# Row maxima of an attention written into the bf16 operand by GpSimd in place of small transfers

## The chip, the cores and the metric

The program runs on one core of one Trainium2 chip, and nothing runs beside it. The metric is the device time of the core in microseconds (us). Before the change the median of three runs is 3215.1 us (3196.7 to 3217.6).

## What is computed

Three layers over x of 2048 positions and 128 channels: a recurrent mixing layer with a mixture-of-experts block behind it, a latent attention, and the same block again. Both blocks (called F and H in the trace) hold a full attention with 16 heads of 8 channels; the latent attention (L) is causal and is brought to the same form. The mixing layer's names begin with R, the experts' with FE and HE. Cut to what matters here:

```python
# F and H: full, once for each of the two blocks
scores = jnp.einsum('bqhd,bkhd->bhqk', q, k) / jnp.sqrt(jnp.float32(Dh))
attn = jax.nn.softmax(scores, axis=-1)
ctx = jnp.einsum('bhqk,bkhd->bqhd', attn, v).reshape(Bb, Ss, Dd)

# L: causal
attn = jnp.einsum('bhql,bkl->bhqk', q_lat, c_kv) / sqrt(hs)
attn = jnp.where(causal[None, None], attn, -jnp.inf)
attn = jax.nn.softmax(attn, axis=-1)
```

The softmax needs the maximum over all keys of each query before the exponential. The kernel computes each score twice: once with the queries on the partitions, to take the maxima, and once with the keys on the partitions, to take the exponential and weigh the values.

## The kernel before

`attention` (lines 89 to 576) is built three times, as F, L and H. Each build has two blocks.

**The first block** (lines 146 to 230) projects queries and keys and splits each float32 into three bf16 parts. The parts go through DRAM (`qscr`, `kscr`) into the operands `qa` and `ka`, 128 partitions by three slots (one for a head) by 2048 columns. A head fills 48 rows (six products of parts by 8 channels), once from partition 0 and once from partition 64, so that two row groups can be multiplied from different rows of the array. GpSimd fills the whole of `ka` with -1 (line 191) and then `vstack` with 1 (line 192); SyncE stores the parts, and issues `load_q` for head 0 once the query parts are stored.

**The second block** (from line 310) runs the heads. A head has 64 max items in F and H (40 in L): TensorE multiplies 128 queries by up to 512 keys into one of three PSUM buffers (line 440), and VectorE reduces it (line 536). It has two halves `a` of 1024 queries. When all maxima of a half are there, VectorE makes `top`, GpSimd splits it into three bf16 parts `topp` (lines 511 to 521, four small operations), TensorE turns `topp` (the "turn" item, line 431), VectorE copies it into `toprow` (line 533), and SyncE writes it with six DMAs (`tops`, lines 316 to 324) into rows 48 to 50 and 112 to 114 of `qa`. `ka` holds -1 there, so that the score matmul over 51 rows (line 401) yields score minus maximum. The first score of each half waits for those DMAs (`top_in`, line 393). ScalarE takes the exponential of 1024 columns (line 497), and TensorE weighs the values (line 419), eight instructions a key tile.

**The order.** Every engine runs its list in order. The max items of the next head are spread between the scores of the current one: `LEAD` (lines 258 to 261) is the number of max items that stand ahead of a head's first score, chosen as the smallest for which each turn lies `MARGIN` cost units ahead of the score that needs it. With 3600, `LEAD` is 44 in F and H, and 42 in L. In L the turn of half 1 of a head and the turn of half 0 of the next head stand 13 items apart; in F and H, 33. TensorE's list loops four times over three heads (line 470), with the first three heads and the last outside the loop. SyncE's list for a head in F and H is: loads of q, k and v two heads on, `spread` (five DMAs for the outputs of the head before), `tops` of half 1, `keep`, `tops` of half 0 of the next head. In the middle of a head VectorE also divides the outputs of the head before (`divide`, lines 547 to 552).

Of the kernel before, what the change touches and what calls it, by code (L numbers as in the profile page):

```python
# [12 lines left out]
P = 128  # L13
# [41 lines left out]
SROWS = MAIN + PARTS  # L55
# [33 lines left out]
def attention(nc, name, xT, wq, wk, wv, consts, out_yT, causal):  # L89
# [3 lines left out]
    zero_rows = consts["zero_rows"]  # L93
    qscr = nc.dram_tensor(name + "_qparts", (PARTS, P + DH, T), BF16, kind="Internal").ap()
# [8 lines left out]
    topp = heads.enter_context(nc.sbuf_tensor(name + "topp", [P, P // 8, 8], BF16))  # L103
# [8 lines left out]
    kept = semaphore(nc, heads, name + "kept")  # L112

    loaded = [semaphore(nc, heads, f"{name}loaded{s}") for s in range(SLOTS)]
    LOADS = 16 * (2 * GROUPS * PARTS + 1)
    FIRST_ROW = [sum(PARTS - b for b in range(a)) * DH for a in range(PARTS)]
# [19 lines left out]
    with ExitStack() as ctx:  # L136
# [17 lines left out]
        with nc.Block() as block:  # L154
# [33 lines left out]
            @block.gpsimd  # L188
            def _(pool):

                nc.gpsimd.memset(ka[:, :, :], -1.0).then_inc(filled, 1)
                nc.gpsimd.memset(vstack[:, :, :, :], 1.0).then_inc(ones, 1)
                nc.gpsimd.memset(topp[:, :, :], 0.0).then_inc(filled, 1)
                nc.gpsimd.memset(nothing[:, :], 0.0).then_inc(filled, 1)
                pool.wait_ge(filled, 3)
# [13 lines left out]
            def _(sp):  # L209
# [8 lines left out]
                sp.sem_inc(kept, 16)  # L218
                for scr in (qscr, kscr):
# [5 lines left out]
                sp.wait_ge(q_stored, 32)  # L225
                load_q(sp, 0, 0)
# [31 lines left out]
    MARGIN = 3600  # L258
# [30 lines left out]
    with heads as ctx:  # L289
# [21 lines left out]
        TOPS = 16 * PARTS * GROUPS  # L311

        with nc.Block() as block:
            @block.sync
            def _(sp):
                def tops(h, a, s, c):

                    sp.wait_ge(max_free, c)
                    for r in range(GROUPS):
                        cols = slice(a * HALF + r * BANK, a * HALF + (r + 1) * BANK)  # L320
                        for part in range(PARTS):
                            row = 64 * r + MAIN + part
                            sp.dma_start(qa[row:row + 1, s, cols].rearrange("o (t q) -> o t q", t=4),
                                         toprow[part * 8 + 4 * r:part * 8 + 4 * r + 4, :]).then_inc(top_in, 16)

# [18 lines left out]
                tops(0, 0, 0, count(0, 0, "turn"))  # L344

                def head(h, u, first=False, last=False):
                    if causal:
                        tops(h, 1, u % SLOTS, count(h, 1, "turn"))
                        if not first:
                            spread(h - 1)  # L350
# [8 lines left out]
                    if not causal:  # L359
                        tops(h, 1, u % SLOTS, count(h, 1, "turn"))  # L360
                    if not first:
                        keep(h - 1)
                    if not last:
                        tops(h + 1, 0, (u + 1) % SLOTS, count(h + 1, 0, "turn"))
# [17 lines left out]
            def _(pe):  # L382
# [7 lines left out]
                def score(h, s, a, n):  # L390

                    if n == 0:
                        pe.wait_ge(top_in, (2 * h + a + 1) * TOPS)
                    done = h * NS + a * NSCORE[0] + n
                    pe.wait_ge(expd, done + 1)
                    for i, (kt, q0, q1) in enumerate(SCORES[a][n]):
                        r = q0 // BANK
                        rows = slice(64 * r, 64 * r + SROWS)
# [25 lines left out]
                def item(h, s, a, j, out, c):  # L424
# [4 lines left out]
                    if j == "turn":  # L429
                        pe.wait_ge(top_split, 2 * h + a + 1)  # L430
                        nc.tensor.transpose(out[:, 0:P // 2].bitcast(BF16), topp[:, :, :].rearrange("p a t -> p (a t)"),
# [5 lines left out]
                    rows = slice(64 * r, 64 * r + MAIN)  # L437
# [72 lines left out]
            def _(pool):  # L510
                def split_maxima(h, a):
                    u = 2 * h + a
                    pool.wait_ge(topped, u + 1)
                    nc.gpsimd.tensor_tensor(topp[:, 0, :], top[:, 0, :], nothing[:, :], ALU.add).then_inc(chain, 1)
# [1155 lines left out]
```

## Time and profile before

| what | us |
|---|---|
| median of three runs | 3215.1 |
| the profiled execution | 3210.3 |
| its span, from first to last instruction | 3208.5 |
| TensorE busy in the span | 2795.7 (87%) |
| VectorE busy | 2123.1 (66%) |
| ScalarE busy | 1714.2 (53%) |
| GpSimd busy | 214.6 (7%) |
| second block of F | 503 to 1262 |
| second block of L | 1585 to 2092 |
| second block of H | 2178 to 2935 |

The three attentions take about 2020 us of the 3208. Busy time of TensorE is modelled and its matmuls overlap. The granted clock is the share of TensorE's full 2.4 GHz; 0.50 is its lower level, 1.2 GHz.

### The profile page before, as it was taken

What the parts mean: (1) busy time and instruction counts of PE and PEld (TensorE: products, weight loads), DVE (VectorE), ACT (ScalarE), POOL (GpSimd) and SP (SyncE); (2) the same over time, 40 slices, a digit from 0 to 9 for tenths busy, and PEclk for the clock granted to TensorE, in tenths of its full rate; (3) what the DMA queues carried; (4) which work ended last, traced back from release to release, by engine and by line L of the source; (5) the groups of instructions that cost most, each with busy time, mean ns of one, the idle gap of its engine ahead of it and who ended that gap; (6) DMA issues with size and microseconds to landing.
All of it is one profiled execution on the core that took longest, in us unless ns stands there. A gap on an engine that the chain in (4) does not pass through costs nothing. (4 is left out here: it accounts for less than half of the span.)

```text
span 3208.5 us, 62945 instructions
## 1 busy us (share of the span) xinstructions
PE 2795.7 (87%) x20985; PEld 1217.1 (38%) x20985; DVE 2123.1 (66%) x4016; ACT 1714.2 (53%) x2055; POOL 214.6 (7%) x469
## 2 busy tenths in 40 slices
PE   6788857999999997999599999939998989896998
PEld 2688842222222232444244444422222223222443
DVE  5544467988888894322578777648988979784222
ACT  4222223776677676433166656624776767675343
POOL 1222210000000000000100000010000000000000
PEclk8888856998898898899699999967989989888999
DMA  1000001110110110211111111110111011010211
GB/s 43 1 0 0 0 17 65 36 33 22 36 35 23 34 36 22 78 41 39 69 40 47 53 38 53 48 65 30 32 36 33 24 35 35 20 36 22 79 59 33
DMA packets 89023, 115.82 MB, mean 36 GB/s; under 512 B 19645, under 2 KB 62615, under 8 KB 86383
## 3 DMA queue, kind: packets, MB, share of 16 engines
q1 hardware_dynamic: 85561, 110.38, 11.2%
q8 instruction: 181, 2.97, 0.4%
q10 hardware_dynamic: 3248, 2.21, 0.3%
q14 instruction: 33, 0.27, 0.0%
HBM read 78.39 MB, written 20.55 MB: 31 GB/s over the span
## 5 line engine op out<-in xcount | busy, mean ns | idle before, releaser
L536 DVE TENSOR_REDUCE Hmaxes<-Hm 128x1 f32<-128x512 f32 x1024 | 626.8, 682 | 108.5 <-PE Hm L440 108.4
L536 DVE TENSOR_REDUCE Fmaxes<-Fm 128x1 f32<-128x512 f32 x1024 | 626.5, 682 | 99.3 <-PE Fm L440 99.3
L497 ACT ACTIVATE Hprob<-Hs 128x1024 f32<-128x1024 f32 x512 | 522.4, 1025 | 208.2 <-PE Hs L401 165.2
L497 ACT ACTIVATE Fprob<-Fs 128x1024 f32<-128x1024 f32 x512 | 522.4, 1025 | 200.7 <-PE Fs L401 158.4
L536 DVE TENSOR_REDUCE Lmaxes<-Lm 128x1 f32<-128x512 f32 (+3 forms) x640 | 354.2, 605 | 111.9 <-PE Lm L440 54.5
L497 ACT ACTIVATE Lprob<-Ls 128x1024 f32<-128x1024 f32 (+7 forms) x384 | 294.1, 777 | 182.3 <-PE Ls L401 99.0
L419 PE MATMUL Fo<-Fprob,Fvh 128*32 128x256 f32 x4096 | 339.9, 419 | 0.3 <-ACT Fprob L497 0.3
L419 PE MATMUL Ho<-Hprob,Hvh 128*32 128x256 f32 x4096 | 337.8, 416 | 0.3 <-ACT Hprob L497 0.3
L440 PE MATMUL Hm<-Hka,Hqa 48*128 48x512 bf16 x1024 | 291.7, 419 | 42.7 <-DVE Hmaxes L536 16.5
L440 PE MATMUL Fm<-Fka,Fqa 48*128 48x512 bf16 x1024 | 294.1, 422 | 38.3 <-DVE Fmaxes L536 15.4
L401 PE MATMUL Hs<-Hqa,Hka 51*128 51x512 bf16 x1024 | 246.6, 407 | 34.6 <-DMA Hqa<-Htoprow 27.6
L401 PE MATMUL Fs<-Fqa,Fka 51*128 51x512 bf16 x1024 | 247.3, 410 | 26.7 <-DMA Fqa<-Ftoprow 25.1
L440 PE MATMUL Lm<-Lka,Lqa 48*128 48x512 bf16 (+3 forms) x640 | 201.9, 377 | 31.6 <-DMA Lvh<-Lvstack 14.2
L419 PE MATMUL Lo<-Lprob,Lvh 128*32 128x256 f32 (+1 forms) x2688 | 211.4, 360 | 0.0
L440 PEld LDWEIGHTS Hm<-Hka,Hqa 48*128 48x128 bf16 x1024 | 83.7, 94 | 312.5 <-DVE Hmaxes L536 152.8
L440 PEld LDWEIGHTS Fm<-Fka,Fqa 48*128 48x128 bf16 x1024 | 84.1, 95 | 310.5 <-DVE Fmaxes L536 157.3
L401 PE MATMUL Ls<-Lqa,Lka 51*128 51x512 bf16 (+3 forms) x640 | 166.0, 362 | 3.4 <-ACT Lprob L497 3.3
L419 PEld LDWEIGHTS Ho<-Hprob,Hvh 128*32 128x32 f32 x4096 | 91.6, 113 | 196.4 <-ACT Hprob L497 106.3
L419 PEld LDWEIGHTS Fo<-Fprob,Fvh 128*32 128x32 f32 x4096 | 92.0, 113 | 190.8 <-ACT Fprob L497 108.2
L794 ACT ACTIVATE FEhid<-FEh,FEb1p 128x512 f32<-128x512 f32 x128 | 87.8, 687 | 124.4 <-PE FEh L749 123.7
L794 ACT ACTIVATE HEhid<-HEh,HEb1p 128x512 f32<-128x512 f32 x128 | 87.6, 687 | 124.3 <-PE HEh L749 123.5
L858 DVE SCALAR_TENSOR_TENSOR HEpart<-HEy,cols,HEwb 128x512 f32<-128x512 f32 x32 | 24.0, 751 | 160.0 <-PE HEy L760 153.2
(426 smaller groups left out, 3072.2 us busy)
## 6 DMA issues: line engine op xcount, KB each, us to landing
FEwb<-FE_weights SPq DMA_DIRECT2D x8, 1024.0 KB, 5.5
HEwb<-HE_weights SPq DMA_DIRECT2D x8, 1024.0 KB, 5.5
Fvh<-Fvstack SPq DMA_DIRECT2D x17, 256.0 KB
Lvh<-Lvstack SPq DMA_DIRECT2D x17, 256.0 KB
Hvh<-Hvstack SPq DMA_DIRECT2D x17, 256.0 KB
FEw<-in_L_ffn_W SPq DMA_DIRECT2D x16, 256.0 KB, 2.9
HEw<-in_L_ffn_W SPq DMA_DIRECT2D x16, 256.0 KB, 2.9
Fqa<-F_qparts SPq DMA_DIRECT2D x34, 96.0 KB
```

What stands on the lines that cost most here:

```text
L401: last = nc.tensor.matmul(sps[n % 2][:, o:o + q1 - q0], ka[rows, s, kt * P:(kt + 1) * P], qa[rows, s, a * HALF + q0:a * HALF + q1], start= ...
L419: last = nc.tensor.matmul(ops[VW * g:VW * (g + 1), j * P:2 * P], vh[:, s, kt * VW:(kt + 1) * VW], p[:, j:2, g * P:(g + 1) * P], start=(kt ...
L440: m = nc.tensor.matmul(out[:, 0:n], qa[rows, s, qt * P:(qt + 1) * P], ka[rows, s, lo:lo + n], start=True, stop=not diag)
L497: nc.scalar.activation(prob[:, :, :].rearrange("p k q -> p (k q)")[:, lo:hi], sps[n % 2][:, o:o + hi - lo], ACT.Exp, scale=SCALE).then_inc ...
L536: nc.vector.reduce_max(maxes[:, a, t, half:half + 1], src[:, 0:w], AX.X).then_inc(max_free, 1)
L794: nc.scalar.activation(hid[:, k % 2, f, :], hps[f][:, :], ACT.Gelu_apprx_tanh, bias=b1p[:, (k // NB) * FC + f:(k // NB) * FC + f + 1])\
L858: nc.vector.scalar_tensor_tensor(out=part[:, k % 2, :], in0=yps[k % YSLOTS][:, :], scalar=b2T[:, bass.ds(i * 2 + u, 1)], in1=wb[:, u, cols ...
```

## The change

Rows. A row group of `qa` and `ka` now begins with twelve rows for the maxima (`TROWS`), four for each part, and the 48 rows of the head follow from row 12. Row 4·part+t holds the maxima in the 128 columns of query tile t of its 512 columns, and zero in the others. Both matmuls run over 60 rows.

Writing. Instead of six DMAs GpSimd multiplies `toprow` (twelve rows, broadcast four times) by `pick` (0 or 1) into 12 rows by 512 columns, twice for each half, once in each row group. The second does not wait for the first.

Clearing. The max matmuls read the maxima's rows too, so those have to be zero before a head's max items. GpSimd clears them for the head two on, with `ka` minus `ka` into 12 rows by 2048 columns, twice for each head (14 heads), in its list between the maxima of half 1 and those of half 0 of the next head. TensorE waits for it (`cleared`) before a head's first max item.

Filling. In the first block GpSimd fills 32 partitions by 6144 columns four times (`ka` and `qa`, each row group) where it filled 128 partitions once, and waits for all four before `vstack`; SyncE waits for them before `load_q` of head 0.

Lead. `MARGIN` becomes 4100 in L, where `LEAD` stays 42 and the order stays, and 5200 in F and H, where `LEAD` becomes 47. SyncE's list loses `tops`.

```diff
-SROWS = MAIN + PARTS
+TROWS = 4 * PARTS
+ROWS = TROWS + MAIN
...
-                nc.gpsimd.memset(ka[:, :, :], -1.0).then_inc(filled, 1)
+                for r in range(GROUPS):
+                    nc.gpsimd.memset(ka[64 * r:64 * r + 32, :, :], -1.0).then_inc(filled, 1)
+                    nc.gpsimd.memset(qa[64 * r:64 * r + 32, :, :], 0.0).then_inc(filled, 1)
+                pool.wait_ge(filled, 4)
                 nc.gpsimd.memset(vstack[:, :, :, :], 1.0).then_inc(ones, 1)
...
                 sp.wait_ge(q_stored, 32)
+                sp.wait_ge(filled, 4)
                 load_q(sp, 0, 0)
...
-    MARGIN = 3600
+    MARGIN = 4100 if causal else 5200
...
-                def tops(h, a, s, c):
-                    sp.wait_ge(max_free, c)
-                    for r in range(GROUPS):
-                        cols = slice(a * HALF + r * BANK, a * HALF + (r + 1) * BANK)
-                        for part in range(PARTS):
-                            row = 64 * r + MAIN + part
-                            sp.dma_start(qa[row:row + 1, s, cols].rearrange("o (t q) -> o t q", t=4),
...
-                        pe.wait_ge(top_in, (2 * h + a + 1) * TOPS)
+                        pe.wait_ge(top_in, (2 * h + a + 1) * GROUPS)
...
-                    rows = slice(64 * r, 64 * r + MAIN)
+                    rows = slice(64 * r, 64 * r + ROWS)
...
+                                pe.wait_ge(cleared, 2 * (h + 1))
...
+                def maxima(h, a, s, c):
...
+                    pool.wait_ge(max_free, c)
+                    for r in range(GROUPS):
+                        rows = slice(64 * r, 64 * r + TROWS)
+                        cols = slice(a * HALF + r * BANK, a * HALF + (r + 1) * BANK)
+                        nc.gpsimd.tensor_tensor(qa[rows, s, cols].rearrange("k (t q) -> k t q", t=4),
+                                                toprow[rows, :].unsqueeze(1).broadcast_to([TROWS, 4, P]),
+                                                pick4(r), ALU.mult).then_inc(top_in, 1)
+                    pool.wait_ge(top_in, GROUPS * (u + 1))
+
+                def clear(h, s):
+
+                    pool.wait_ge(weighed, RING + NK * h)
+                    for r in range(GROUPS):
+                        rows = slice(64 * r, 64 * r + TROWS)
+                        nc.gpsimd.tensor_tensor(qa[rows, s, :], ka[rows, s, :], ka[rows, s, :], ALU.subtract)\
+                            .then_inc(cleared, 1)
+                    pool.wait_ge(cleared, 4 + GROUPS * h)
+
+                def head(h, u, first=False, last=False):
+                    maxima(h, 1, u % SLOTS, count(h, 1, "turn"))
+                    if not first and not last:
+                        clear(h, (u + 2) % SLOTS)
+                    if not last:
+                        maxima(h + 1, 0, (u + 1) % SLOTS, count(h + 1, 0, "turn"))
```

A table `pick` of four columns is loaded with the other constants and copied to bf16 once.

## Rows read from the trace of the kernel before

**Rows 1.** The page's costliest groups: the score matmuls of H; idle before, releaser.

```profile
L401 PE MATMUL Hs<-Hqa,Hka 51*128 51x512 bf16 x1024 | 246.6, 407 | 34.6 <-DMA Hqa<-Htoprow 27.6
```

**Rows 2.** Busy time in stretches: two heads of F, two of L; clock behind POOL.

```profile
631.10:674.10 43.00, 40.49 (x391) 12.36 (x387) 40.63 (x70) 33.16 (x35) 1.61 (x8) 1.00 0.10 31
910.80:959.50 48.70, 43.63 (x387) 13.74 (x386) 40.77 (x70) 33.20 (x35) 1.60 (x8) 0.89 0.11 32
1735.20:1764.20 29.00, 28.14 (x316) 12.88 (x314) 23.89 (x49) 18.73 (x26) 1.61 (x8) 1.00 0.18 50
1764.20:1800.30 36.10, 32.22 (x316) 14.62 (x314) 24.10 (x48) 18.89 (x26) 1.60 (x8) 0.86 0.15 42
```

**Rows 3.** Timeline (start, length, instruction) of VectorE: half 0's maxima, heads 1 and 16.

```profile
546.06 0.18 DVE L544 TENSOR_REDUCE Ftop<-Fmaxes 128x8 f32<-128x32 f32 x1
...
1238.68 0.19 DVE L544 TENSOR_REDUCE Ftop<-Fmaxes 128x8 f32<-128x32 f32 x1
...
2211.20 0.19 DVE L544 TENSOR_REDUCE Htop<-Hmaxes 128x8 f32<-128x32 f32 x1
...
2912.24 0.19 DVE L544 TENSOR_REDUCE Htop<-Hmaxes 128x8 f32<-128x32 f32 x1
```

**Rows 4.** Timeline of TensorE: first scores of half 1 in two heads of F.

```profile
638.74 0.39 PE L401 MATMUL Fs<-Fqa,Fka 51*128 51x512 bf16 x2 [0.53 <-DMA Fqa<-Ftoprow]
...
729.29 0.39 PE L401 MATMUL Fs<-Fqa,Fka 51*128 51x512 bf16 x2 [1.00 <-DMA Fqa<-Ftoprow]
```

**Rows 5.** Timeline ahead of the second of them: the copy, and SyncE's six DMAs.

```profile
723.68 0.22 DVE L533 COPY Ftoprow<-Fm 128x128 bf16<-128x128 bf16 x1
...
724.29 3.86 SPq L323 DMA_DIRECT2D Fqa<-Ftoprow  x6
```

**Rows 6.** Timeline of VectorE: the division in a head's middle, the reduction behind it.

```profile
637.68 0.94 DVE L549 RECIPROCAL Fsums<-Fsums 128x128 f32<-128x128 f32 x1
...
638.98 1.28 DVE L536 TENSOR_REDUCE Fmaxes<-Fm 128x1 f32<-128x512 f32 x2
```

**Rows 7.** Timeline of VectorE: a max item behind the first score of half 0.

```profile
618.86 1.29 DVE L536 TENSOR_REDUCE Fmaxes<-Fm 128x1 f32<-128x512 f32 x2 [0.36 <-PE Fm L440]
```

**Rows 8.** Timeline of the first block of F: GpSimd's fill, SyncE's first loads.

```profile
469.54 5.22 POOL L191 MEMSET Fka<- 128x6144 bf16 x1 [55.28 <-POOLq L592]
...
482.92 3.95 SPq L124 DMA_DIRECT2D Fqa<-F_qparts  x6
...
496.42 3.89 SPq L132 DMA_DIRECT2D Fka<-F_kparts  x6
```

**Rows 9.** Groups by form: elementwise work on GpSimd, and on VectorE with 64 partitions and 128.

```profile
L1000 POOL TENSOR_TENSOR RvT<-RvT,Rmix_k 128x2048 f32<-128x2048 f32 x1 | 4.5, 4519 | 0.1
L1110 POOL TENSOR_TENSOR RXT<-RMB,tab 128x512 f32<-128x512 f32 x8 | 10.2, 1270 | 191.6 <-DVE RMB L1188 191.6
L1169 DVE SCALAR_TENSOR_TENSOR RAR<-Rkk,RT 64x512 f32<-64x512 f32 x8 | 5.5, 686 | 0.2
L1206 DVE TENSOR_TENSOR RX<-Rq,RX 128x512 f32<-128x512 f32 x32 | 22.1, 692 | 67.9 <-PE Rq L1241 67.9
```

**Rows 10.** Timeline of GpSimd: two fills with no wait between them.

```profile
0.28 0.10 POOL L1658 MEMSET const-float32-1.0<- 128x1 f32 x1
0.32 0.10 POOL L1658 MEMSET const-bfloat16-1.0<- 128x1 bf16 x1
```

**Rows 11.** Timeline of L: from the turn of half 1 to the next head's turn.

```profile
1699.45 0.23 DVE L533 COPY Ltoprow<-Lm 128x128 bf16<-128x128 bf16 x1
...
1706.45 0.20 POOL L514 TENSOR_TENSOR Ltopp<-Ltop,Lnothing 128x8 bf16<-128x8 f32 x1 [8.12 <-DVE Ltop L542]
...
1707.29 0.20 POOL L520 TENSOR_TENSOR Ltopp<-Ltop,Ltopp 128x8 bf16<-128x8 f32 x1
...
1708.36 0.23 PE L431 MATMUL Lm<-ident_bf,Ltopp 128*128 128x128 bf16 x1 [0.29 <-DVE Lmaxes L536]
```

**Rows 12.** Timeline of TensorE: its loop's second pass in L begins.

```profile
1787.62 0.22 PE L440 MATMUL Lm<-Lka,Lqa 48*128 48x128 bf16 x1 [3.09 <-issue]
```

More of the change, by code:

```diff
@@ L93, in attention @@
     zero_rows = consts["zero_rows"]
+    pick = consts["pick_bf"]
     qscr = nc.dram_tensor(name + "_qparts", (PARTS, P + DH, T), BF16, kind="Internal").ap()
@@ L102, in attention @@
     ka = heads.enter_context(nc.sbuf_tensor(name + "ka", [P, SLOTS, T], BF16))
-    topp = heads.enter_context(nc.sbuf_tensor(name + "topp", [P, P // 8, 8], BF16))
+    topp = heads.enter_context(nc.sbuf_tensor(name + "topp", [P, GROUPS, P // 8, 4], BF16))
     nothing = heads.enter_context(nc.sbuf_tensor(name + "nothing", [P, 8], F32))
@@ L112, in attention @@
     kept = semaphore(nc, heads, name + "kept")
+    cleared = semaphore(nc, heads, name + "cleared")
     loaded = [semaphore(nc, heads, f"{name}loaded{s}") for s in range(SLOTS)]
     LOADS = 16 * (2 * GROUPS * PARTS + 1)
-    FIRST_ROW = [sum(PARTS - b for b in range(a)) * DH for a in range(PARTS)]
+    FIRST_ROW = [TROWS + sum(PARTS - b for b in range(a)) * DH for a in range(PARTS)]
     def load_q(sp, h, s):
@@ L218, in _ @@
                 sp.sem_inc(kept, 16)
+                sp.sem_inc(cleared, 4)
                 for scr in (qscr, kscr):
@@ L343, in _ @@
                     load_kv(sp, h, h)
-                tops(0, 0, 0, count(0, 0, "turn"))
                 def head(h, u, first=False, last=False):
[L347 to L350, printed above, removed]
+                    if causal and not first:
+                        spread(h - 1)
                     if not last:
@@ L436, in item @@
                     r = kb % GROUPS
-                    rows = slice(64 * r, 64 * r + MAIN)
+                    rows = slice(64 * r, 64 * r + ROWS)
                     lo = kb * BANK
@@ L510, in _ @@
             def _(pool):
-                def split_maxima(h, a):
+                pick4 = lambda r: pick[64 * r:64 * r + TROWS, :].unsqueeze(2).broadcast_to([TROWS, 4, P])
+                def maxima(h, a, s, c):
                     u = 2 * h + a
+                    halves = lambda x: x.rearrange("p (r t) -> p r t", r=GROUPS)
+                    high, middle, low = (topp[:, :, part, :] for part in range(PARTS))
                     pool.wait_ge(topped, u + 1)
-                    nc.gpsimd.tensor_tensor(topp[:, 0, :], top[:, 0, :], nothing[:, :], ALU.add).then_inc(chain, 1)
+                    nc.gpsimd.tensor_tensor(high, halves(top[:, 0, :]), halves(nothing[:, :]), ALU.add).then_inc(chain, 1)
@@ L515, in split_maxima @@
                     pool.wait_ge(chain, u * 3 + 1)
-                    nc.gpsimd.tensor_tensor(top[:, 1, :], top[:, 0, :], topp[:, 0, :], ALU.subtract).then_inc(chain, 1)
+                    nc.gpsimd.tensor_tensor(halves(top[:, 1, :]), halves(top[:, 0, :]), high, ALU.subtract)\
+                        .then_inc(chain, 1)
                     pool.wait_ge(chain, u * 3 + 2)
-                    nc.gpsimd.tensor_tensor(topp[:, 1, :], top[:, 1, :], nothing[:, :], ALU.add).then_inc(chain, 1)
+                    nc.gpsimd.tensor_tensor(middle, halves(top[:, 1, :]), halves(nothing[:, :]), ALU.add).then_inc(chain, 1)
@@ L519, in split_maxima @@
                     pool.wait_ge(chain, u * 3 + 3)
-                    nc.gpsimd.tensor_tensor(topp[:, 2, :], top[:, 1, :], topp[:, 1, :], ALU.subtract)\
-                        .then_inc(top_split, 1)
-                with pool.Fori(0, NH) as h:
-                    for a in range(2):
-                        split_maxima(h, a)
+                    nc.gpsimd.tensor_tensor(low, halves(top[:, 1, :]), middle, ALU.subtract).then_inc(top_split, 1)
+                    pool.wait_ge(max_free, c)
[5 more added lines that the diff above has]
+                                                pick4(r), ALU.mult).then_inc(top_in, 1)
@@ L527, in _ @@
+                maxima(0, 0, 0, count(0, 0, "turn"))
+                for u in range(SLOTS):
+                    head(u, u, first=(u == 0))
+                with pool.Fori(1, (NH - 1) // SLOTS) as i:
+                    for u in range(SLOTS):
+                        head(i * SLOTS + u, u)
+                head(NH - 1, 0, last=True)
             @block.vector
@@ L1432 @@
 CONSTS = [("ident", P), ("eye2", HS), ("mpair", 2 * P), ("levels", LEVELS * P), ("level0t", P), ("blockones", P),
-          ("iota", E_N)]
+          ("iota", E_N), ("pick", 4)]
 MASKS = [("ident2", 2 * P), ("mask2_kq", 2 * P), ("mask2_qk", 2 * P)]
@@ L1457, in constant_table @@
         "mask2_qk": folded(np.where(r > c, BIG, 0.0)),
+        "pick": np.where(r % 64 < TROWS, r % 4 == np.arange(4)[None, :], 0.0),
         "iota": np.broadcast_to(np.arange(E_N)[None, :], (P, E_N)),
@@ L1532, in build @@
         consts["ident_bf"] = sb("ident_bf", [P, P], BF16)
+        consts["pick_bf"] = sb("pick_bf", [P, 4], BF16)
         for n in ("ident2_bf", "mask2_kq_bf", "mask2_qk_bf"):
```

18 lines of the change are left out of this document (6 added, 12 removed).

## The prediction

> **What bounds the kernel now.** I read the costliest groups first, to see what TensorE waits for. In H its score matmuls sit idle for 27.6 us behind the DMAs that bring the maxima [rows 1]; F shows 25.1 us, L nothing. That is under 1 us a half, and by itself small. So I looked next at single heads, in the stretches. A head of F at full clock takes 43.0 us, with VectorE busy for 40.6 of it: VectorE, with its 64 reductions, sets the pace, and TensorE at 40.5 us is just behind it [rows 2]. But most heads are not like this one. From head 1's maxima to head 16's, fifteen heads take 692.6 us in F and 701.0 us in H [rows 3], where fifteen of 43.0 would take 645. The reader is to ask where those 48 and 56 us are.
>
> Part is the clock. At the lower level TensorE can't keep VectorE fed. The timeline of TensorE shows when the level falls: the score that opens half 1 waited 0.53 us in an early head, which stayed at full clock, and 1.00 us in a later one [rows 4], and the 9.5 us behind that were granted 0.50. I listed these waits in F as far as the timeline prints them: nine were of 1.00 to 2.21 us, and eight of the nine were followed by a stretch at 0.50 (six of 9 to 10 us, two shorter); three of 0.53 to 0.61 us were followed by none. The wait is long because SyncE is late: the copy into `toprow` ended at 723.90, and the six DMAs began at 724.29 and took 3.86 us to issue [rows 5], behind the loads and `spread`.
>
> The other part is TensorE's loop. Three times in each attention, as its list jumps back, TensorE pauses for some 3.1 us with nothing to wait for [rows 12] and the clock falls behind it. Such a head costs 48.7 us in F (its half 1 kept the full clock), against 43.0, so 5.7 more; in L 36.1 against 29.0, so 7.1 more [rows 2].
>
> **The change part by part, in F and H.** It removes the DMAs and their wait. What stands in their place: GpSimd's two multiplications of 12 by 512. No row shows twelve partitions or bf16 there; the nearest is 1.27 us for 128 by 512 f32 [rows 9]. From the copy's end that makes 0.1 + 2.5 us if one runs behind the other, against 5.4 us from 723.90 to 729.29 [rows 4, 5], and the longer lead gives three max items more, about 1.9 us by 0.64 us an item (1.28 us for two, [rows 6]). So the maxima are there some 4.5 us earlier than now, against waits of at most 2.2 us. The wait is gone. What is late next is the division: VectorE leaves its reductions at 637.68 and comes back at 638.98 [rows 6], and TensorE, three buffers ahead at most, stands still for part of that. It did so in the early head with its wait of 0.53 us, and that head kept its clock [rows 2, 4]. So I take the clock to stay up in half 1 as well. In half 0 a gap of 0.36 us on VectorE goes [rows 7].
>
> A head then takes 43.0 - 0.36 = 42.6 us. Fifteen make 639.0, less 1.0 because the first of them has no division, plus three loop pauses at 5.7 = 17.1: 655.1 us. Against 692.6 and 701.0 [rows 3] that saves 37.5 us in F and 45.9 in H, 83.4 together. The lead costs at the end: the scores trail the last maximum by three items more, 1.9 us each in F and H, 3.8 together. Net 79.6, say 80 us. The bounds: if the wait goes and the lower clock stays, about 30 us (see the rivals); if the loop pauses too lost their low stretch, 5.7 would become 3.1 and six of them give 16 us more.
>
> The clearing, 12 by 2048, is by the nearest row 4.5 us [rows 9], twice. In F and H the next turn's maxima come 28 max items after the copy, over 17 us, and 2.5 + 9.0 us fit in front. Its wait for `weighed` is over by then, and TensorE's wait for `cleared` comes almost a head later. Nothing is queued on GpSimd that anyone needs sooner. 60 rows in place of 48 and 51 stream the same number of columns: nothing. SyncE loses 576 DMA issues in all; it isn't what ends the steady heads once `top_in` doesn't hang on it, and its loads, two heads ahead, come no later: nothing. `pick` costs one small copy at the start: nothing.
>
> **In L** no wait for the maxima exists to be removed and the order stays, so there is only something to lose. Here the clearing sits in a narrow place. The copy of half 1 ended at 1699.68; GpSimd's split for the next head ran from 1706.45 to 1707.49, and TensorE took the turn at 1708.36 [rows 11], 8.7 us behind the copy. Between them GpSimd now has two multiplications, two clearings and the split (1.0 us). If operations on different partitions run one behind the other: 0.1 + 2.5 + 0.1 + 9.0 + 1.1 = 12.8 us, 4.1 us late, and TensorE, in order, stands at the turn with every score, weighing and max item behind it. If the two of a pair overlap: 0.1 + 1.3 + 0.1 + 4.5 + 1.1 = 7.1 us, 1.6 us early, and nothing is lost. So the whole question is whether they overlap. What the trace shows: a fill at 0.28 of 0.10 us, and the next one starting at 0.32 [rows 10], so GpSimd's sequencer doesn't wait for one to end before it starts the next; and these have no semaphore between them, as the new pairs have none. It doesn't show a pair on different partitions. I take the overlap, as the nearer to this row, and keep the other end as a rival.
>
> The Trainium skill's GPSIMD Engine Reference, section 2.1 (Instruction dispatch), says why it could: each of the engine's eight cores serves its own 16 partitions and starts the next instruction once its own share is done, without waiting for the others. Rows 0 to 11 and 64 to 75 belong to different cores, so by that rule the pair costs 4.5 us and L loses nothing, and by a strict order it costs 9.0 us; no row of this trace shows partial partitions on GpSimd, so it stays a rule until one does. The same rule lets no part of a single instruction go faster with twelve partitions than with sixteen.
>
> **The first block.** One fill of 6144 columns takes 5.22 us [rows 8]. Four of 32 partitions: 20.9 us if they run in order with the cost of the whole, 10.4 us if the row groups overlap, 5.2 us or less if the cost goes by partitions (on VectorE 64 partitions cost 686 ns and 128 692 ns [rows 9], so I don't take that for GpSimd either). SyncE would issue `load_q` at 482.92, 13.4 us behind the start of the fill [rows 8]. With 10.4 us it isn't delayed; with 20.9 us it is by 7.5 us, and all that follows up to 496.42 is issued by SyncE one behind the other, so the second block begins 7.5 us later, three times: 22.5 us. `vstack` follows, later than now, but ends before SyncE does in both cases. I take 0, by the same answer as in L.
>
> **The sum.** 3208.5 - 80 = 3128.5 us of span. The profiled execution took 3210.3 us and the median of the runs is 3215.1; 80 off the median is 3135 us, 2.5% less.
>
> **The rivals.** *In order.* GpSimd runs the pairs one behind the other. L: in eleven of the fourteen heads with a clearing TensorE stands for 4.1 us, and the pause of 3.09 us, which cost 7.1 us [rows 2, 12], shows that it doesn't end there: the clock falls and 4.0 us more go. 8.1 × 11 = 89 us; at the three loop pauses the gap is wider already, some 1 us each; together 92. With the 22.5 of the first blocks that is 115 against 80 saved: 3250 us, slower. For it speaks that no row shows an overlap of different partitions; against it the two fills [rows 10]. It decides from where the clearings take more than some 6 us together (8.7 less 0.1, 1.3, 0.1 and 1.1): below that L is untouched.
>
> *The clock stays low.* The wait goes, but the division and the three idle pieces around it still bring the lower level, as one shorter mechanism in half 1. Then only the waits are saved: 0.36 us in half 0 and about 0.9 us in half 1, in some 27 heads, 34, less 3.8: 30 us, 3185. Against it stands the early head, which had the division and stayed up; for it, that the later heads differ in the loads beside them.
>
> *No change at all*, the maxima as late as now because a broadcast, masked write on GpSimd costs several times its nearest row: from 1.27 us each it would have to be 3.5 us in order. Then 3215.
>
> **How the numbers follow.** The forecast (overlap, clock kept) 0.50, its own range 3108 to 3170; the clock stays low 0.22; in order 0.20; no change or a mixture 0.08. A difference under 1%, 32 us, is about what a measurement of this kernel can't tell from none. Faster by over 1%: 0.50, half of the second case and 0.01 of the last, 0.62. Within 1%: the other half and most of the last, 0.17. Slower: 0.21. The range goes from 3108 (forecast with 16 us for the loops and some 10 for the other terms) to 3235, which leaves out most of the in-order case.
>
> **What would show it.** Right: no wait of a score on the maxima; heads of F near 42.6 us at clock 1.00 but for three with a pause; in GpSimd's timeline the second of a pair starting while the first runs; in L 29.0 us a head as before; `load_q` of head 0 no later behind the fill than 13.4 us. Wrong: the turn in L idle behind the split with GpSimd's clearings ahead of it, or fills at a distance of 5.2 us; or stretches of 0.50 in the middle of the heads of F with no wait for maxima ahead of them.

## The result, and the profile after

The change makes the kernel slower: 3329.0 us (median of four runs, 3319.2 to 3335.2) against 3213.0 us (four runs of the kernel before, 3196.7 to 3217.6), a ratio of 1.037, with a 95% interval of 1.032 to 1.041. The forecast was 3135 us, and its range ended at 3235. The profiled execution took 3329.6 us with a span of 3327.9, and its mean granted clock is 0.867 against 0.883 before.

To see where the 119.4 us of span come from, I cut both spans at the first and the last max matmul of each attention. One row a matmul group gives both (shortest, median and longest duration, then first and last start). First the kernel before, then after:

```profile
L440 PE MATMUL Fm<-Fka,Fqa x1024: 372/387/632, 502.8 to 1237.4; 48*128 48x512 bf16 x171
...
L440 PE MATMUL Hm<-Hka,Hqa x1024: 372/387/632, 2167.6 to 2911.0; 48*128 48x512 bf16 x171
...
L440 PE MATMUL Lm<-Lka,Lqa x640: 224/386/631, 1584.4 to 2065.7; 48*128 48x512 bf16 x127, 48*128 48x128 bf16 x16, 48*128 48x384 bf16 x16, 48*128 48x256 bf16 x1
```

```profile
L428 PE MATMUL Fm<-Fka,Fqa x1024: 383/387/631, 507.9 to 1276.9; 60*128 60x512 bf16 x171
...
L428 PE MATMUL Hm<-Hka,Hqa x1024: 376/387/631, 2262.0 to 3031.1; 60*128 60x512 bf16 x171
...
L428 PE MATMUL Lm<-Lka,Lqa x640: 223/386/631, 1629.7 to 2154.2; 60*128 60x512 bf16 x127, 60*128 60x128 bf16 x16, 60*128 60x384 bf16 x16, 60*128 60x256 bf16 x1
```

F grew from 734.6 to 769.0 us, L from 481.3 to 524.5, H from 743.4 to 769.1, and all that lies outside them from 1249.2 to 1265.3: +34.4, +43.2, +25.7 and +16.1, together 119.4. So it isn't one place.

What the change was made for did happen. In the page's costliest groups the score matmuls of H were idle for 34.6 us before [rows 1]; after, no DMA stands among the releasers. A new wait stands in another group, the max matmuls of F, which wait for VectorE's reductions:

```profile
L428 PE MATMUL Fm<-Fka,Fqa 60*128 60x512 bf16 x1024 | 317.1, 431 | 89.4 <-DVE Fmaxes L558 59.9
...
L389 PE MATMUL Hs<-Hqa,Hka 60*128 60x512 bf16 x1024 | 262.2, 409 | 1.7 <-ACT Hprob L486 1.7
```

The list of TensorE's waits in F counts them (waiter, releaser: us, times, longest): 59.9 us, with one as long as 3.4 us.

```profile
PE Fm L428 <- DVE Fmaxes L558: 59.9, 71, 3.4
```

The timeline of the middle of a head of F shows what VectorE does there (start, length, instruction, idle time before it):

```profile
693.20 7.26 POOL L530 TENSOR_TENSOR Fqa<-Fka 12x2048 bf16<-12x2048 bf16 x2 [0.17 <-POOL Fqa L520]
...
696.53 0.95 DVE L571 RECIPROCAL Fsums<-Fsums 128x128 f32<-128x128 f32 x1
...
697.62 2.98 DVE L574 TENSOR_TENSOR Fquot<-Fsums 128x128 f32<-128x128 f32 x1
700.52 3.07 DVE L558 TENSOR_REDUCE Fmaxes<-Fm 128x1 f32<-128x512 f32 x5
701.26 1.20 PE L428 MATMUL Fm<-Fka,Fqa 60*128 60x512 bf16 x2 [3.42 <-DVE Fmaxes L558]
```

GpSimd's two clearings run from 693.20 to 700.46. The quotient, a multiplication of 128 by 128 with both operands in SBUF, starts inside them and is over only at 700.60, right behind their end: 2.98 us. Before, it took 0.29 us. The reciprocal (one operand) keeps its 0.95 us inside the same clearings, and the reductions, whose operand is in PSUM, keep their 0.6 us each. It is so in most heads: the median of 16 is 2980 ns. The quotient's line in before, in F after, and in L after (where it doesn't meet the clearings):

```profile
L552 DVE TENSOR_TENSOR Fquot<-Fsums x16: 291/292/293, 595.8 to 1271.1; 128x128 f32<-128x128 f32 x16
```

```profile
L574 DVE TENSOR_TENSOR Fquot<-Fsums x16: 291/2980/2985, 601.6 to 1309.3; 128x128 f32<-128x128 f32 x16
...
L574 DVE TENSOR_TENSOR Lquot<-Lsums x16: 291/291/295, 1703.0 to 2188.5; 128x128 f32<-128x128 f32 x16
```

TensorE, in order, stands still for 3.42 us, and the clock falls behind it. The first stretch is a whole head of F, the second the 9.8 us in which the wait ends (the clock is the third figure from the end); the third is a head of L. They answer to the heads of 43.0 us at 1.00 and 29.0 us at 1.00 before [rows 2].

```profile
667.40:715.40 48.00, 43.73 (x391) 13.58 (x394) 43.25 (x71) 33.26 (x34) 12.91 (x14) 0.89 0.10 30
700.00:709.80 9.80, 8.54 (x48) 2.24 (x48) 7.27 (x12) 4.43 (x5) 0.45 (x1) 0.50 0.03 8
...
1716.65:1749.94 33.29, 30.61 (x316) 13.07 (x314) 24.39 (x48) 18.86 (x26) 12.91 (x14) 0.90 0.14 43
```

In L it is the other case, the rival called "in order". GpSimd's timeline, and the turn behind it:

```profile
1719.43 2.14 POOL L520 TENSOR_TENSOR Lqa<-Ltoprow,pick_bf 12x512 bf16<-12x512 bf16 x2 [1.35 <-DVE Ltoprow L555]
1721.64 7.26 POOL L530 TENSOR_TENSOR Lqa<-Lka 12x2048 bf16<-12x2048 bf16 x2
1728.98 0.20 POOL L507 TENSOR_TENSOR Ltopp<-Ltop,Lnothing 128x8 bf16<-128x8 f32 x1
...
1729.81 0.20 POOL L514 TENSOR_TENSOR Ltopp<-Ltop,Ltopp 128x8 bf16<-128x8 f32 x1
1730.16 0.22 PE L419 MATMUL Lm<-ident_bf,Ltopp 128*128 128x128 bf16 x1 [2.41 <-POOL Ltopp L514]
```

The groups give the mean of one as 1031 and 3591 ns, so two take 2.14 and 7.26 us: one behind the other, with no overlap to be seen. The turn is 2.41 us late, and a head of L takes 33.3 us.

The first block of F shows the same pattern:

```profile
466.85 5.21 POOL L195 MEMSET Fka<- 32x6144 bf16 x1 [55.04 <-POOLq L614]
472.01 5.21 POOL L196 MEMSET Fqa<- 32x6144 bf16 x1
477.27 5.21 POOL L195 MEMSET Fka<- 32x6144 bf16 x1
482.44 5.21 POOL L196 MEMSET Fqa<- 32x6144 bf16 x1
...
487.74 3.98 SPq L127 DMA_DIRECT2D Fqa<-F_qparts  x6
```

The fills start every 5.2 us, and `load_q` is issued 20.9 us behind the first of them, against 13.4 us before [rows 8].

### The profile page after: what moved, and what is told of

It reads as the page before. It is cut to its first block and busy times, and to the rows that moved or that the text cites. A ratio compares the mean times of both kernels' runs of the same rounds, so it can differ in the third digit from the quotient of the medians.

```text
span 3327.9 us, 62702 instructions
## 1 busy us (share of the span) xinstructions
PE 2834.5 (85%) x20985; PEld 1218.5 (37%) x20985; DVE 2200.0 (66%) x4017; ACT 1714.6 (52%) x2055; POOL 760.6 (23%) x754
## 3 DMA queue, kind: packets, MB, share of 16 engines
q8 instruction: 182, 2.98, 0.4%
## 5 line engine op out<-in xcount | busy, mean ns | idle before, releaser
L428 PE MATMUL Hm<-Hka,Hqa 60*128 60x512 bf16 x1024 | 312.7, 427 | 101.6 <-DVE Hmaxes L558 62.0
L428 PE MATMUL Fm<-Fka,Fqa 60*128 60x512 bf16 x1024 | 317.1, 431 | 89.4 <-DVE Fmaxes L558 59.9
L389 PE MATMUL Fs<-Fqa,Fka 60*128 60x512 bf16 x1024 | 266.5, 414 | 1.7 <-ACT Fprob L486 1.7
L389 PE MATMUL Hs<-Hqa,Hka 60*128 60x512 bf16 x1024 | 262.2, 409 | 1.7 <-ACT Hprob L486 1.7
L428 PE MATMUL Lm<-Lka,Lqa 60*128 60x512 bf16 (+3 forms) x640 | 208.2, 399 | 35.8 <-DMA Lvh<-Lvstack 21.6
L428 PEld LDWEIGHTS Hm<-Hka,Hqa 60*128 60x128 bf16 x1024 | 87.2, 95 | 375.8 <-DVE Hmaxes L558 188.9
L428 PEld LDWEIGHTS Fm<-Fka,Fqa 60*128 60x128 bf16 x1024 | 87.4, 95 | 369.0 <-DVE Fmaxes L558 188.2
L407 PE MATMUL Lo<-Lprob,Lvh 128*32 128x256 f32 (+1 forms) x2688 | 219.4, 373 | 0.0
L389 PE MATMUL Ls<-Lqa,Lka 60*128 60x512 bf16 (+3 forms) x640 | 183.1, 391 | 3.4 <-ACT Lprob L486 3.2
```

What stands on the lines that cost most here:

```text
L389: last = nc.tensor.matmul(sps[n % 2][:, o:o + q1 - q0], ka[rows, s, kt * P:(kt + 1) * P], qa[rows, s, a * HALF + q0:a * HALF + q1], start= ...
L407: last = nc.tensor.matmul(ops[VW * g:VW * (g + 1), j * P:2 * P], vh[:, s, kt * VW:(kt + 1) * VW], p[:, j:2, g * P:(g + 1) * P], start=(kt ...
L428: m = nc.tensor.matmul(out[:, 0:n], qa[rows, s, qt * P:(qt + 1) * P], ka[rows, s, lo:lo + n], start=True, stop=not diag)
```

## The experiments

Theory A: two mechanisms together make the loss, and each can be taken away alone. In F and H the clearing holds VectorE's quotient, and the clock falls behind it; in L, and in the first blocks, GpSimd runs its pairs in order. The rivals are that the loss of F and H comes from something else that the change brought (60 rows instead of 51, the order of SyncE's list, the longer lead), or that the half clock would come anyway. Two of the kernels, before + clearings and before + fills, add work on a tile that nobody reads.

The clearing moved behind the next head's first maxima, 13 items later in L and 33 in F and H (against the changed kernel, as are the next three):

```diff
                     maxima(h, 1, u % SLOTS, count(h, 1, "turn"))
-                    if not first and not last:
-                        clear(h, (u + 2) % SLOTS)
                     if not last:
                         maxima(h + 1, 0, (u + 1) % SLOTS, count(h + 1, 0, "turn"))
+                    if not first and not last:
+                        clear(h, (u + 2) % SLOTS)
```

> The changed kernel with one thing moved: in GpSimd's list the clearing stands behind the maxima of half 0 of the next head, not ahead of them. Theory A (the clearing does the harm by its place: in L it delays the split that the turn waits for; in F and H it lies across VectorE's quotient, a tensor_tensor with two SBUF inputs, which then takes 2.98 us for 0.29 and leaves TensorE standing for 3.4 us): the quotient is back at 0.29 us in F and H, TensorE's wait of 3.42 us is gone, L's heads go from 33.6 back to 29.0 us, and the whole takes some 3225 us. Theory B (the clearing loads SBUF or the power budget wherever it stands, or 60 rows and the longer lead are what costs): L gains its 40 us, F and H nothing, 3285 us.

Measured: 3181.0 us, 0.989 [0.987, 0.991] of before. F is 692.1 us and H 703.5, which is 42.5 and 39.9 less than before and 77 and 66 less than with the change. The quotient is back at 292 ns there. The expectation had some 3225 us, 44 more than came, and L's heads back at 29.0 us, which didn't come: the moved clearings now meet L's quotient, and it takes 2.35 us there.

```profile
1717.85 7.26 POOL L530 TENSOR_TENSOR Lqa<-Lka 12x2048 bf16<-12x2048 bf16 x2 [0.17 <-POOL Lqa L520]
...
1719.22 2.37 DVE L574 TENSOR_TENSOR Lquot<-Lsums 128x128 f32<-128x128 f32 x1
```

In this place the quotient is let go 3.7 us into the 7.26 (1721.59 against 1717.85), at the end of the first of the two clearings (half of 7.26 is 3.63). So it waits for the one instruction that runs when it comes, not for the pair. L is 512.0 us, still 30.7 more than before.

The other side moved, the division six scores later in F and H, with the clearing where the change put it:

```diff
-                        if k == NS // 2 and not first:
+                        if k == NS // 2 + (0 if causal else 6) and not first:
```

> The changed kernel with VectorE's division six score items later in the heads of F and H (at item 22 of 32, not 16), so that it stands some 8 us behind its old place and outside the clearing; GpSimd's list, L and the first blocks are those of the changed kernel. Theory A: the quotient takes 0.29 us, F and H lose 25 to 30 us each against the changed kernel, L stays at 524 us: 3265 to 3280 us. Theory B (contention wherever, rows, lead): 3329 us, with the quotient short but the heads of F still near 48 us.

Measured: 3187.5 us, 0.991 [0.989, 0.993]. F 694.0, H 700.1, and L at 524.3, as slow as with the change. The work is the same, and so are the rows, SyncE's list, the lead and the number of clearings; only where the division stands differs. It brings back 144 us in F and H together (75.0 and 69.0). The median fell by 141 us, more than twice the 49 to 64 that I expected. The 25 to 30 us that I expected for each attention are about 2 us for each of its 14 heads with a clearing, and some 5 us a head came back: the clock's part was missing, and the mean clock of the whole went from 0.867 to 0.900, above the 0.883 of before. The rivals for F and H are out.

The clearing given to SyncE, as two DMAs of zeros for each head:

```diff
+        for r in range(GROUPS):
+            sp.dma_start(qa[64 * r:64 * r + TROWS, s, :], zero_rows[0:TROWS, :]).then_inc(loaded[s], 16)
...
-                    if not first and not last:
-                        clear(h, (u + 2) % SLOTS)
```

> The changed kernel without GpSimd's clearing: the twelve rows of each group are zeroed by two DMAs from a DRAM tensor of zeros, ahead of the loads of q. Theory A: as with the clearing moved, some 3225 us; the two should agree within 10 us, since the clearing behind the next head's maxima touches nothing that waits. Theory B (the clearing costs wherever it stands): clearly faster than with the clearing moved, 3200 us or less.

Measured: 3159.4 us, 0.982 [0.979, 0.985]. F 694.5, L 478.6, H 708.2: both mechanisms gone with the clearings. The expectation was missed: this kernel was to lie within 10 us of the one with the clearing moved, and it is 21.6 us faster, below the 3200 us named for the theory that a clearing costs wherever it stands. But F and H are no faster than with the clearing moved (692.1 and 703.5). The difference is L, 33.4 us, where the moved clearing holds the quotient, less 7.1 in F and H and 6.9 outside. So a clearing costs where it meets a quotient or comes ahead of a turn, and not wherever it stands. What lies outside the attentions' heads is 1276.1 us, though, 26.9 more than before.

The collision put into the kernel before, which has none of the rest: two such operations a head, 28 in each attention, on a spare tile.

```diff
+                def clear(h):
+                    pool.wait_ge(max_free, count(h, 1, "turn"))
+                    for r in range(GROUPS):
+                        rows = slice(64 * r, 64 * r + 12)
+                        nc.gpsimd.tensor_tensor(spare[rows, 0, :], spare[rows, 1, :], spare[rows, 1, :], ALU.subtract)\
+                            .then_inc(cleared, 1)
```

> The kernel before with 28 operations of the clearing's form (12 partitions by 2048 bf16, on a spare tile that nothing reads) added to GpSimd's list in each attention, in pairs behind the turn of half 1 in 14 heads. Nothing waits for them but GpSimd. Theory A: the quotient takes 2 us or more in F and H and the time goes up by 30 to 70 us, to 3245 to 3285; in L the pair ends just ahead of the turn, so that its heads stay near 29 us. Rival (the port isn't shared with such an instruction; the quotient is long in the changed kernel for another reason): the quotient stays at 0.29 us and the time at 3213 us.

Measured: 3275.9 us, 1.019 [1.016, 1.021]. F +30.8, H +33.7, L −0.5. The timeline in F, and the quotient's line:

```profile
737.70 3.59 POOL L529 TENSOR_TENSOR Fspare<-Fspare 12x2048 bf16<-12x2048 bf16 x1
738.91 2.52 DVE L569 TENSOR_TENSOR Fquot<-Fsums 128x128 f32<-128x128 f32 x1
...
L569 DVE TENSOR_TENSOR Fquot<-Fsums x16: 293/2527/2543, 596.4 to 1301.9; 128x128 f32<-128x128 f32 x16
```

The quotient ends at 741.43, the operation beside it at 741.29. So such subtractions alone, without anything else of the change, make F and H slower. L isn't touched here, and that fits the space of 8.7 us [rows 11]: without the multiplications GpSimd's list there is 0.1 + 7.3 + 1.0 = 8.4 us.

The same place in the kernel before, but with fills (12 by 4096, so that they last as long: 7.06 us for two). The diff is against the kernel with the clearings put in; a small operation ahead of the fills carries the wait:

```diff
-                        nc.gpsimd.tensor_tensor(spare[rows, 0, :], spare[rows, 1, :], spare[rows, 1, :], ALU.subtract)\
-                            .then_inc(cleared, 1)
+                        nc.gpsimd.memset(spare[rows, :, :], 0.0).then_inc(cleared, 1)
...
```

> The kernel before with pairs of GpSimd fills of 12 partitions by 4096 bf16 on a spare tile, where e9_before_clears had tensor_tensor of 12 by 2048, at the same place and about as long (3.5 us each). It tells which operation of GpSimd holds VectorE's quotient up. If what they share is the way in (two operands read from SBUF), a fill, which reads nothing, leaves the quotient at 0.29 us and the time near 3217 us. If it is the engine's way out or any instruction of GpSimd, the quotient takes 2 us or more, as with the clearings, 3270 us.

Measured: 3210.1 us, 1.000 [0.997, 1.003].

```profile
727.49 7.06 POOL L531 MEMSET Fspare<- 12x4096 bf16 x2
...
732.24 0.29 DVE L570 TENSOR_TENSOR Fquot<-Fsums 128x128 f32<-128x128 f32 x1
```

The quotient runs in the middle of the fills and takes 0.29 us. The fill, which only writes, doesn't hold it; the subtraction, which reads two operands from SBUF, does.

So the change's own clearing as a fill (a small operation ahead of it carries the wait):

```diff
-                        nc.gpsimd.tensor_tensor(qa[rows, s, :], ka[rows, s, :], ka[rows, s, :], ALU.subtract)\
-                            .then_inc(cleared, 1)
+                        nc.gpsimd.memset(qa[rows, s, :], 0.0).then_inc(cleared, 1)
...
```

> The changed kernel with the clearing at its place but written as a fill with zero (12 partitions by 2048, some 1.8 us each by the 0.85 ns a column of the other fills), behind one small operation that carries the wait. It reads nothing and takes half as long. Theory A: the quotient is 0.29 us in F and H although the clearing stands where it stood, the split in L is not late (2.2 + 0.3 + 3.6 + 1.1 = 7.2 us against 8.7), and the time is that of e1_clear_dma or a little less, 3150 to 3160 us. Rival (what hurts is work of GpSimd at that place, of whatever kind): 3180 us or more.

Measured: 3148.4 us, 0.981 [0.978, 0.983]. F 695.1, L 477.1, H 701.3. A fill of 12 by 2048 takes 1.8 us where the subtraction took 3.6, so it fits in L too.

The first blocks, on the kernel that clears by DMA: two fills of 128 partitions for four of 32.

```diff
-                for r in range(GROUPS):
-                    nc.gpsimd.memset(ka[64 * r:64 * r + 32, :, :], -1.0).then_inc(filled, 1)
-                    nc.gpsimd.memset(qa[64 * r:64 * r + 32, :, :], 0.0).then_inc(filled, 1)
+                nc.gpsimd.memset(ka[:, :, :], -1.0).then_inc(filled, 1)
+                nc.gpsimd.memset(qa[:, :, :], 0.0).then_inc(filled, 1)
...
```

> The changed kernel with the clearing by two DMAs (as in e1_clear_dma) and with the operands filled in the first block by one fill of 128 partitions for ka and one for qa, in place of four fills of 32 partitions. Theory: a fill costs by its columns (5.2 us for 32 and for 128 partitions), so the four took 20.8 us and two take 10.4; SyncE's loads of head 0 start at once when the query parts are stored, and each attention starts 5 to 8 us earlier than in e1_clear_dma: 3135 to 3145 us, faster than both kernels. Rival (the first blocks end by something else, such as the projections or the wait for the key parts): no change against e1_clear_dma, 3159 us.

Measured: 3137.5 us, 0.977 [0.971, 0.982], 21.9 us less than with four fills. What lies outside the attentions' heads went from 1276.1 to 1254.8 us.

The lead, taken alone. First the long one in the kernel before:

```diff
-    MARGIN = 3600
+    MARGIN = 3600 if causal else 5200
```

> The kernel before with MARGIN 5200 in F and H (47 max items ahead), L as before, transfers as before. Theory (waits of 1.0 to 2.2 us for the maxima's DMAs bring TensorE's lower clock, and without them a head of F takes 42.6 to 43 us): the lead of 1.9 us more takes most of the wait away, F and H lose 25 to 35 us each, 3150 to 3175 us. Rival (the clock falls in the middle of a head because of the division or the loads beside it): the wait is gone, the stretches at half clock stay, 3200 us or more.

Measured: 3191.5 us, 0.994 [0.992, 0.997]. The maxima's DMAs are still waited for, for 14.6 us in F and 18.1 in H instead of 25.1 and 27.6. F falls by 16.4 us and H by 6.1. The expectation of 3150 to 3175 us was missed: three more items aren't enough to get rid of the wait. It comes 12 times in F and 10 times in H in place of 29 each, and is still up to 2.2 and 2.7 us long. It tells that part of the gain could be had without the change, and leaves open how much a still longer lead would bring.

```profile
L401 PE MATMUL Hs<-Hqa,Hka 51*128 51x512 bf16 x1024 | 255.2, 405 | 20.4 <-DMA Hqa<-Htoprow 18.1 <-ACT Hprob L497 2.3
```

Then the short one (3600 everywhere) behind the fills and the clearing by DMA:

> e11_dma_fills with MARGIN 3600 as before, so that 44 max items stand ahead of the first score in F and H, not 47. If the longer lead is what removes the wait, the scores wait for the maxima again and the clock falls behind it: 3170 us or more. If GpSimd's quicker way (2.2 us from the copy on, against 5.4 for the DMAs) is enough by itself, the wait stays away and the time is that of e11_dma_fills or up to 4 us less.

Measured: 3124.4 us, 0.973 [0.967, 0.978], 13 us below the kernel with the long lead, where the lead's tail alone was to give 0 to 4. The scores still don't wait for the maxima; their group in F, as the trace lists it:

```profile
L390 PE MATMUL Fs<-Fqa,Fka 60*128 60x512 bf16 x1024 | 241.4, 391 | 1.7 <-ACT Fprob L486 1.7
```

The first fill of F starts at 467.30 us in this profile and at 472.79 in the other, so 5.5 us of it lie in the mixing layer, ahead of everything that the two kernels do differently. The rest, 6.8 us of span, is 5.5 outside the heads and 1.3 inside. The intervals of the two ratios overlap, but the executions don't (3119.8 to 3131.6 against 3136.3 to 3140.5 us), so a gain is likely, and its cause stays open. What is sure is that the long lead wasn't needed.

Last, all that helped together: clearing by fills, two fills in the first block, the short lead.

> The same, with the two fills of 128 partitions in the first block and MARGIN 3600 in all three attentions (44 max items ahead in F and H). Theory: the gains of the three add up: e4_clear_memset less some 20 us for the fills and some 10 us for the lead, without the 32 DMAs for each attention of e13_dma_fills_lead44: 3115 to 3130 us. If the wait for the maxima comes back with the short lead, 3150 us or more.

Measured: 3123.6 us (3121.0 to 3127.1), 0.973 [0.970, 0.975] of the kernel before. In L, where the change was late, GpSimd's list now ends in time, and it even waits 0.61 us for VectorE ahead of the split:

```profile
1710.89 2.14 POOL L520 TENSOR_TENSOR Lqa<-Ltoprow,pick_bf 12x512 bf16<-12x512 bf16 x2 [1.42 <-DVE Ltoprow L555]
...
1713.33 3.65 POOL L531 MEMSET Lqa<- 12x2048 bf16 x2
1717.59 0.20 POOL L507 TENSOR_TENSOR Ltopp<-Ltop,Lnothing 128x8 bf16<-128x8 f32 x1 [0.61 <-DVE Ltop L564]
```

All of them side by side, F to outside in us of the profiled span, cut as above. A ratio compares a kernel with executions of the kernel before taken beside it (medians from 3208.1 to 3217.8), so it isn't exactly the quotient of two medians of the table:

| kernel | F | L | H | outside | median | ratio |
|---|---|---|---|---|---|---|
| before | 734.6 | 481.3 | 743.4 | 1249.2 | 3213.0 | 1 |
| the change | 769.0 | 524.5 | 769.1 | 1265.3 | 3329.0 | 1.037 |
| clearing later | 692.1 | 512.0 | 703.5 | 1269.2 | 3181.0 | 0.989 |
| division later | 694.0 | 524.3 | 700.1 | 1268.7 | 3187.5 | 0.991 |
| clearing by DMA | 694.5 | 478.6 | 708.2 | 1276.1 | 3159.4 | 0.982 |
| before + clearings | 765.4 | 480.8 | 777.1 | 1249.9 | 3275.9 | 1.019 |
| before + fills | 732.6 | 481.5 | 747.0 | 1255.0 | 3210.1 | 1.000 |
| clearing by fills | 695.1 | 477.1 | 701.3 | 1272.7 | 3148.4 | 0.981 |
| by DMA, two fills | 697.6 | 476.0 | 707.8 | 1254.8 | 3137.5 | 0.977 |
| before, long lead | 718.2 | 480.0 | 737.3 | 1249.9 | 3191.5 | 0.994 |
| by DMA, two fills, short lead | 698.7 | 475.3 | 706.1 | 1243.8 | 3124.4 | 0.973 |
| by fills, two fills, short lead | 693.1 | 478.3 | 708.9 | 1239.4 | 3123.6 | 0.973 |

## Why the prediction was wrong

**The bound, and the waits for the maxima: right.** The waits are gone, and the head of F without a collision takes what was forecast, 42.6 us at full clock. One such head, of the kernel that clears by DMA and fills twice:

```profile
642.77:685.44 42.67, 40.42 (x386) 12.68 (x386) 40.49 (x72) 33.12 (x35) 5.73 (x12) 1.00 0.13 36
```

The fifteen heads were forecast at 655.1 us. In that kernel they take 656.5 us in F and 667.9 in H (two rows of the timeline of VectorE for each, as in [rows 3]):

```profile
550.35 0.19 DVE L564 TENSOR_REDUCE Ftop<-Fmaxes 128x8 f32<-128x32 f32 x1
...
1206.83 0.19 DVE L564 TENSOR_REDUCE Ftop<-Fmaxes 128x8 f32<-128x32 f32 x1
...
2173.14 0.19 DVE L564 TENSOR_REDUCE Htop<-Hmaxes 128x8 f32<-128x32 f32 x1
...
2841.01 0.19 DVE L564 TENSOR_REDUCE Htop<-Hmaxes 128x8 f32<-128x32 f32 x1
```

These rows, like the four of [rows 3], belong to half 1, the second of a head, and not to half 0 as [rows 3] has it. Fifteen heads lie between them either way.

That the clock comes back once the score doesn't wait was right in the main: the mean is 0.907 there. The rival "the clock stays low" isn't wholly out. In this same kernel TensorE waits 0.72 to 1.31 us for VectorE's reductions behind each division, and in 6 of 28 heads (three in F, three in H) a stretch at 0.50 follows, with no wait for maxima ahead of it. The prediction named that as a sign of being wrong. One such head of H, its wait, and the head as a whole:

```profile
2532.11 1.20 PE L429 MATMUL Hm<-Hka,Hqa 60*128 60x512 bf16 x2 [1.10 <-DVE Hmaxes L556]
...
2500.59:2546.91 46.32, 44.23 (x391) 13.74 (x393) 40.73 (x71) 33.26 (x34) 5.73 (x12) 0.89 0.11 33
```

H's 12.8 us over the forecast are such heads and the three with a loop pause, which took 49.4 to 51.0 us where 42.6 + 5.7 = 48.3 was forecast. The prediction's list of waits also lacks one: in the kernel before, a wait of 0.64 us at 967.32 was followed by a stretch at 0.50.

**The step that failed most: "Nothing is queued on GpSimd that anyone needs sooner", for F and H.** I laid the clearings beside GpSimd's own list and found room for 9.0 us. I didn't lay them beside VectorE's list, where the quotient stands in the same few microseconds: the copy of half 1 and the division are both in the middle of the head. VectorE doesn't wait for GpSimd by any semaphore there, so neither the code nor the waits of before show a link. With the change the fifteen heads take 728.0 us in F (the same two rows, in the kernel after) and 729.4 in H by the same rows:

```profile
550.70 0.19 DVE L566 TENSOR_REDUCE Ftop<-Fmaxes 128x8 f32<-128x32 f32 x1
...
1278.67 0.19 DVE L566 TENSOR_REDUCE Ftop<-Fmaxes 128x8 f32<-128x32 f32 x1
```

That is 72.9 and 74.3 us over 655.1, together 147 of the 199 us by which the span (3327.9) missed the forecast (3128.5). A head pays 5.0 us (48.0 against 43.0): 2.7 us of a held quotient on the engine that sets the pace, and the rest where the clock falls behind TensorE's 3.42 us. Moving either of the two operations takes it away, adding the clearings to the kernel before brings it, and writing the same zeros by a fill at the same place doesn't. That shows the cause. The size of the term, had I seen it: the quotient held for up to one subtraction (4.5 us by [rows 9], 3.6 as measured) is a pause like the loop's 3.09 us [rows 12]. By the 5.7 us that such a pause cost a head of F [rows 2], 28 times 5.7 is 160 us, and the sign would have turned.

The rule was to be had. The Trainium skill's SBUF — State Buffer (section "SBUF: two separate sides") states that a VectorE instruction with two SBUF inputs and a GpSimd instruction that reads SBUF exclude each other: whichever starts first has the ports for its whole length, and the other stands fully blocked. The traces agree where GpSimd is first: 2.98 us in place of 0.29, let go within 0.14 us of the end of the subtraction, and no effect of a fill. No run here shows GpSimd held by VectorE.

**"I take the overlap": wrong, and with it L and the first blocks.** Of the two ends that I kept, the wrong one was chosen. The row of two fills 0.04 us apart [rows 10] shows that two small operations can be recorded close together; it isn't evidence for two long ones on different partitions. The pairs took 2.14 us for two of 1.03 and 7.26 for two of 3.59, and the fills of 5.21 us start 5.2 us apart: in each case the sum. The rival "in order" is what happened in L, and its terms can be checked: from the copy's end to the turn it had 12.8 us, and it is 10.8 (1719.34 to 1730.16), since a clearing takes 3.6 us and not 4.5, and a multiplication 1.03 and not 1.27; so TensorE stands for 2.4 us at the turn and not for 4.1, and the clock's part is 1.9 us a head and not 4.0. L lost 43.2 us where the rival had 92. The first blocks were well sized: the rival had 7.5 us each, 22.5 together. From the first fill to F's first max matmul it is 41.1 us against 33.3, 7.8 more. In L it is 40.6 against 33.2 and in H 40.6 against 34.9, by these rows of the first fills (before, then after) and the first max matmuls above, so 20.8 us in all. Two fills for four brought 21.3 us back outside the heads.

```profile
1551.18 5.22 POOL L191 MEMSET Lka<- 128x6144 bf16 x1 [255.86 <-POOLq L592]
2132.69 5.22 POOL L191 MEMSET Hka<- 128x6144 bf16 x1 [64.36 <-POOLq L592]
...
1589.11 5.21 POOL L195 MEMSET Lka<- 32x6144 bf16 x1 [255.82 <-POOLq L614]
2221.42 5.21 POOL L195 MEMSET Hka<- 32x6144 bf16 x1 [61.72 <-POOLq L614]
```

The Trainium skill's GPSIMD Engine Reference, section 2.1, on which I leaned for the overlap, speaks of eight cores that each start the next instruction on their own; no pair here shows it, and the measurement decides.

**How it adds up.** By the cut at the max matmuls F was to fall by 37.5 us and grew by 34.4, 71.9 off; H was to fall by 45.9 and grew by 25.7, 71.6 off; L is 43.2 off. The first blocks are 20.8 off. All the rest outside was to grow by the lead's 3.8 us and fell by 4.7, of which 2.7 are a mixing layer that ended earlier: 8.5 the other way. Together that is the 199 us that were missed. The rival that came closest in number, 3250 us, had the right mechanism for L but would have been wrong in F and H, where 80 us of gain stood in its sum.

**Costs of nothing:** 60 rows were nothing (max matmuls at 387 ns, as before). SyncE's shorter list shows no cost, but no run takes it alone. **The masked multiplication** costs 1.03 us, a little under its nearest row of 1.27 [rows 9]. **The lead** was charged with 3.8 us; the tail itself was never separated, and the two kernels that differ in it differ by 13, of which 5.5 lie ahead of it.

## What to carry to other kernels

Lay each new operation of GpSimd that reads SBUF beside VectorE's list as well as its own, and look for a VectorE operation with both operands in SBUF under it; move one of them, or write the value with a fill, which reads nothing. Count two GpSimd operations on different partitions as one behind the other until a trace shows otherwise. And where the engine that sets the pace is 94% busy, as VectorE in a head here, count about twice a stall of 3 us on it: the 2.7 us of the held quotient cost a head of F 5.0, since TensorE's clock falls behind it.

## What the runs showed of the hardware

- VectorE's 128 by 128 multiplication with two SBUF operands went from 0.29 to 2.98, 2.52 and 2.35 us in three kernels, each time to the end of the GpSimd subtraction of 12 by 2048 that was running (in the third by half of the pair's 7.26 us). GpSimd didn't lose by it: 7.26 us a pair with and without a quotient in it. That twelve partitions hold up an operation on 128 was not expected. VectorE's reciprocal (0.95 us) and its reductions from PSUM (0.6 us) are untouched.
- A fill on GpSimd doesn't hold the quotient (0.29 us inside a pair of 7.06), and goes by columns: 6144 in 5.21 us for 32 partitions and 5.22 for 128, 2048 in 1.8 us for 12. A fill of 12 by 2048 is half the price of the subtraction that writes the same zeros.
- A wait of TensorE of 3.42 us was followed by 9.8 us at a granted clock of 0.50, in a head that is otherwise at full clock.
